# Queries and keys of one attention layer: normalised, scaled, turned and saved group by group in one pipeline

## What is computed

```python
x = x + _L0_attn_ref(_layernorm(x), ...)
x = x + _L0_ffn_ref(_layernorm(x), ...)
qkv = _layernorm(x) @ qkv_w + qkv_b                     # 128 -> 3 * 128
q, k, v = jnp.split(qkv, 3, axis=-1)                    # 16 heads of 8 channels
q = q / (jnp.linalg.norm(q, axis=-1, keepdims=True) + 1e-06) * qn_scale + qn_bias
k = k / (jnp.linalg.norm(k, axis=-1, keepdims=True) + 1e-06) * kn_scale + kn_bias
for _ in range(2):                                      # the training steps
    grads = jax.grad(loss)(theta)      # loss = mean((swish(k @ gate) * (k @ val) @ proj - v) ** 2)
    theta = muon(theta, grads)
x = x + (swish(q @ gate) * (q @ val)) @ proj @ proj_w + proj_b
x = x + _L1_ffn_ref(_layernorm(x), ...)                 # eight experts, two for each token
```

## Time and profile before

| | us |
|---|---|
| three runs | 1463.47 median, 1460.00 to 1467.11 |
| the profiled execution, its own time | 1465.41 |
| its span, first to last instruction | 1463.7 |
| PE busy in the span | 1172.7 (80%) |
| DVE busy | 939.5 (64%) |
| ACT busy | 446.6 (31%) |
| POOL busy | 507.3 (35%) |
| mean granted clock of PE | 0.905 of 2.4 GHz |
| the stage of the change, first transpose to the first training matmul | 504.97 to 597.73 |

### The profile page before, as it was taken

The page is one execution under the profiler, slowest core; times in us unless marked ns, Lnnn a source line. Parts: engine busy times, 40 slices in busy tenths (PEclk is TensorE's granted clock), DMA queues, the critical chain, the costliest instruction groups (busy, mean ns, idle before and its releaser), DMA issues.

```text
span 1463.7 us, 16561 instructions
## 1 busy us (share of the span) xinstructions
PE 1172.7 (80%) x4825; PEld 699.6 (48%) x4825; DVE 939.5 (64%) x2037; ACT 446.6 (31%) x844; POOL 507.3 (35%) x461
## 2 busy tenths in 40 slices
PE   3899999905656564699999889999988997399990
PEld 1444444403345432355555555555555665277770
DVE  5787888775577699467667556766754665323324
ACT  3545444235322231222122322212232322133340
POOL 4788888922244156400000000000000366245552
PEclk9999999957977785699999999999999998599995
DMA  4312222000000003100008200000000112434415
GB/s 134 107 56 63 76 63 77 1 0 1 1 0 0 1 0 137 65 22 22 14 21 355 74 0 22 22 14 21 8 15 7 44 50 68 125 87 112 121 46 183
DMA packets 60188, 81.82 MB, mean 56 GB/s; under 512 B 8620, under 2 KB 34622, under 8 KB 59617
## 3 DMA queue, kind: packets, MB, share of 16 engines
q1 hardware_dynamic: 55201, 72.54, 15.6%
q0 software_dynamic: 4672, 8.55, 1.8%
q10 hardware_dynamic: 256, 0.03, 0.0%
HBM read 33.77 MB, written 31.99 MB: 45 GB/s over the span
## 4 chain that ended last, share of the span: by engine, by line
PE 65%; DVE 16%; issue 8%; POOL 4%; ACT 4%; DMA 1%; SPq 1%; DVEq 0%; POOLq 0%; ACTq 0%
PE banks L1516 45%; PE banks L1405 7%; PE banks L1551 2%; PE banks L1337 2%; PE banks L1338 2%; PE banks L1493 1%; DVE arena L1990 1%; PE banks L1467 1%; DVE X L1878 1%; PE banks L1346 1%; POOL arena L936 1%; DVE arena L1798 1%; ACT XN L1158 1%; POOL arena L971 1%; DVE q_small L649 1%
## 5 line engine op out<-in xcount | busy, mean ns | idle before, releaser
L1516 PE MATMUL banks<-arena 128*128 128x128 f32 (+4 forms) x1516 | 391.5, 397 | 7.6 <-DVE arena L2084 4.5
L1516 PEld LDWEIGHTS banks<-arena 128*128 128x128 f32 (+1 forms) x1516 | 208.8, 191 | 89.2 <-issue 61.6
L1405 PE MATMUL banks<-arena,ident 128*128 128x512 f32 x368 | 175.3, 609 | 10.3 <-DVE arena L1829 9.0
L1022 POOL IOTA arena<- 128x32 f32 x1 | 0.2, 205 | 510.2 <-DVE ttt_val_w L2091 510.2
L2029 DVE TENSOR_TENSOR arena<-banks,arena 128x512 f32<-128x512 f32 x64 | 44.2, 691 | 134.4 <-ACT arena L1228 134.4
L936 POOL TENSOR_TENSOR arena<-arena 128x512 f32<-128x512 f32 x96 | 112.2, 1195 | 16.8 <-ACT arena L1095 16.8
L1054 POOL DMA_INDIRECT expert_out_scratch<-arena x80 | 80.6, 1007 | 97.1 <-DVE arena L2286 76.0
L1405 PEld LDWEIGHTS banks<-arena,ident 128*128 128x128 f32 x368 | 67.7, 194 | 88.2 <-issue 64.9
L1829 DVE TENSOR_TENSOR arena<-arena,banks 128x512 f32<-128x512 f32 x152 | 96.1, 675 | 0.5 <-PE banks L1405 0.5
L943 POOL TENSOR_TENSOR arena<-arena 128x512 f32<-128x512 f32 x64 | 81.3, 1270 | 5.0
L1231 ACT ACTIVATE arena<-banks 128x512 f32<-128x512 f32 x64 | 38.2, 597 | 146.5 <-PE banks L1551 146.5
(11 more groups left out here) (316 smaller groups left out, 2122.7 us busy)
## 6 DMA issues: line engine op xcount, KB each, us to landing
arena<-arena SPq DMA_DIRECT2D x64, 224.0 KB
arena<-expert_in_scratch SPq DMA_DIRECT2D x16, 580.5 KB
expert_in_scratch<-arena SPq DMA_DIRECT2D x4, 1225.5 KB
expert_in_scratch<-arena SPq DMA_DIRECT2D x5, 967.5 KB
arena<-kT_scratch SPq DMA_DIRECT2D x16, 256.0 KB, 2.6
arena<-k_scratch SPq DMA_DIRECT2D x16, 256.0 KB, 2.6
arena<-in_L_ffn_W_dram SPq DMA_DIRECT2D x16, 256.0 KB, 3.0
arena<-expert_out_scratch SPq DMA_DIRECT2D x8, 512.0 KB, 6.8
```

The source lines that it names most:

```text
L1405: m = nc.tensor.matmul(bank[ACC[b % 2]][:], ident[:], src, start=first, stop=last)
L1516: return nc.tensor.matmul(out_, lhsT, rhs, start=start, stop=stop)
```

## The change

The three parts become one pipeline over iterations 0 to 11, written out without loops. In iteration i: VectorE adds the bias of group i and normalises group i-2 (`unit`: the seven small steps, now on 128 columns, and the wide multiply). ScalarE normalises the tiles of group i+1 (`normalised5`), copies them when turned, takes the root of group i-1, squares group i, copies out the turned key and query of group i-3 and the key of group i-4. TensorE multiplies group i, turns the key and query of group i-3 straight from `QK`, and turns the key of group i-4 back.

Scale and bias move behind the turn. There a channel is a partition, so that ScalarE's copy takes them as its scale and bias operands, from the four columns of `affine`. They are made once: four copies on VectorE into `tiled4`, four transposes, one small copy. Since k is now finished only in turned form, TensorE turns it back (bank 1) and ScalarE copies it to `kBs`, from where it is saved.

SP waits, before the first load, for the last group's saves to be issued but only for group 0's to have landed. POOL loses the two steps on the queries; its additions of `b_proj` follow the last head sums directly. `kTs`, `qTs`, `kBs` and `nrm` have space of their own. `xT5` turns through one bank (0) instead of two.

```diff
-        kTs = xs5
-        qTs = xT5
+        kTs = view(o5, 2, L)
+        qTs = view(o5 + 2 * L, 2, L)
+        kBs = view(o5 + 4 * L, 2, L)
+        nrm = view(o5, 2, 6, TPB * NH2)
+        tiled4 = view(o5, 4, P)
+        affine = sb("affine", P, 4)
...
@@ sync @@
-            by_pairs(sp, NB, save_qk)
-            for s in range(2):
-                for x in (k_saved, kT_saved, qT_saved):
-                    sp.wait_ge(x[s].sem, x[s].at(NB // 2))
+            for g in range(NB + 1):
+                if g < NB:
+                    save(kT_dram, kTs, kT_ready, kT_saved, g)
+                    save(qT_dram, qTs, qT_ready, qT_saved, g)
+                if g:
+                    save(k_dram, kBs, kB_ready, k_saved, g - 1)
...
+                    for g in range(NB):
+                        sp.wait_ge(kT_saved[g % 2].sem, kT_saved[g % 2].at(g // 2 + 1))
+                        sp.wait_ge(k_saved[g % 2].sem, k_saved[g % 2].at(g // 2 + 1))
+                        load_k(g, g % 2)
...
@@ gpsimd @@
-            def q_affine(g, s):
-                pool.tensor_tensor(out=qv, in0=qv, in1=q_scale[:].unsqueeze(1).unsqueeze(1).to_broadcast(sh), op=ALU.mult).then_inc(q_scaled.sem, q_scaled.unit)
-                pool.tensor_tensor(out=qS[:, s, :].rearrange("p (c h d) -> p c h d", c=TPB, d=HD), in0=qv,
-                                              in1=q_bias[:].unsqueeze(1).unsqueeze(1).to_broadcast(sh), op=ALU.add).then_inc(q_ready.sem, q_ready.unit)
-            by_pairs(pool, NB, q_affine)
...
@@ scalar @@
+            def turned_kq(g):
+                act.wait_ge(kqT_mm.sem, kqT_mm.at(2 * g + 1))
+                nc.scalar.activation(kTs[:, g % 2, :], bank[6][:], ACT.Identity, bias=affine[:, 1:2], scale=affine[:, 0:1]).then_inc(kT_ready.sem, kT_ready.unit)
+                act.wait_ge(kqT_mm.sem, kqT_mm.at(2 * g + 2))
+                nc.scalar.activation(qTs[:, g % 2, :], bank[7][:], ACT.Identity, bias=affine[:, 3:4], scale=affine[:, 2:3]).then_inc(qT_ready.sem, qT_ready.unit)
+            for i in range(NB + 4):
+                if i + 1 < NB:
+                    normalised5(i + 1)
+                    xT5_copy(i + 1)
+                if 1 <= i <= NB:
+                    root(i - 1)
+                if i < NB:
+                    squares(i)
+                if 3 <= i < NB + 3:
+                    turned_kq(i - 3)
+                if 4 <= i:
+                    turned_back(i - 4)
...
@@ tensor @@
+            for i in range(NB + 4):
+                if i < NB:
+                    pe.wait_ge(xT5_ready.sem, xT5_ready.at(i + 1))
+                    for j in range(TPB):
+                        if j == TPB - 1 and i + 1 < NB:
+                            xT5_transposes(i + 1)
+                        if i:
+                            pe.wait_ge(v_biased.sem, v_biased.at((i - 1) * TPB + j + 1))
+                        nc.tensor.matmul(bank[2 + j][:, 0:3 * D], xT5[:, i % 2, j * P:(j + 1) * P], w_qkv[:], start=True, stop=True).then_inc(qkv_mm.sem, qkv_mm.unit)
+                if 3 <= i < NB + 3:
+                    turn_kq(i - 3)
+                if 4 <= i:
+                    turn_k_back(i - 4)
...
@@ vector @@
+            for i in range(NB + 2):
+                if i < NB:
+                    bias_qkv(i)
+                if i >= 2:
+                    unit(i - 2)
```

More of the change, by code:

```diff
@@ L1187, in _, with normalised5 @@
             layernorm_root(act, 4)
-            def xT5_copy(g, s):
+            def normalised5(g):
+                if g >= 2:
+                    act.wait_ge(xT5_mm.sem, xT5_mm.at(g - 1))
+                for j in range(TPB):
+                    n = g * TPB + j
+                    nc.scalar.activation(xs5[:, g % 2, j * P:(j + 1) * P], X[:, n, :], ACT.Identity,
+                                         bias=shift[:, n:n + 1], scale=rstd[:, n:n + 1]).then_inc(ln["out"].sem, ln["out"].unit)
@@ L1217, in _, with root @@
[L1217 to L1221 removed]
+                nc.scalar.activation(SQ[:, g * TPB:(g + 1) * TPB, :], QK[:, g * TPB:(g + 1) * TPB, :], ACT.Square).then_inc(qk_squared.sem, qk_squared.unit)
+            def root(g):
+                act.wait_ge(sum_sq_ready.sem, sum_sq_ready.at(g + 1))
+                if g >= 2:
+                    act.wait_ge(nrm_step.sem, nrm_step.at(7 * (g - 2) + 2))
+                nc.scalar.activation(nrm[:, g % 2, 0, :], sum_sq[:, g * TPB * NH2:(g + 1) * TPB * NH2], ACT.Sqrt).then_inc(root_ready.sem, root_ready.unit)
@@ L1475, in _ @@
             m.then_inc(wpT_mm.sem, wpT_mm.unit)
+            pe.wait_ge(wide_made.sem, wide_made.at(4))
+            for i in range(4):
+                m = nc.tensor.transpose(bank[4][:, i * P:(i + 1) * P], tiled4[:, i, :], ident[:])
+            m.then_inc(affine_mm.sem, affine_mm.unit)
             pe.wait_ge(x2_ready.sem, x2_ready.at(NB))
             pe.wait_ge(wpT_ready.sem, wpT_ready.at(1))
-            def xT5_transposes(g, s):
+            pe.wait_ge(affine_ready.sem, affine_ready.at(1))
@@ L1485, in xT5_transposes @@
                 m.then_inc(xT5_mm.sem, xT5_mm.unit)
-            def qkv(g, s, last=False):
-                pe.wait_ge(xT5_ready.sem, xT5_ready.at(g + 1))
-                for j in range(TPB):
-                    if j == TPB - 1 and not last:
-                        xT5_transposes(g + 1, 1 - s)
-                    pe.wait_ge(v_biased.sem, v_biased.at((g - 1) * TPB + j + 1))
-                    nc.tensor.matmul(bank[2 + j][:, 0:3 * D], xT5[:, s, j * P:(j + 1) * P], w_qkv[:], start=True, stop=True).then_inc(qkv_mm.sem, qkv_mm.unit)
@@ L1510, in _, with turn_kq @@
-            by_pairs(pe, NB, transposes)
-            pe.wait_ge(kT_ready.sem, kT_ready.at(NB))
+            def turn_kq(g):
+                pe.wait_ge(unit_ready.sem, unit_ready.at(g + 1))
+                for part, (at_, to, done) in enumerate(((D, 6, kT_ready), (0, 7, qT_ready))):
+                    if g:
+                        pe.wait_ge(done.sem, done.at(g))
+                    for j in range(TPB):
+                        m = nc.tensor.transpose(bank[to][:, j * P:(j + 1) * P], QK[:, g * TPB + j, at_:at_ + D], ident[:])
+                    m.then_inc(kqT_mm.sem, kqT_mm.unit)
@@ L1939, in _ @@
                 nc.vector.bn_stats(stats[:, n, :], X[:, n, :]).then_inc(ln["stats"].sem, ln["stats"].unit)
+            for i, v in enumerate((k_scale, k_bias, q_scale, q_bias)):
+                nc.vector.tensor_copy(tiled4[:, i, :].rearrange("p (h d) -> p h d", d=HD), v[:].unsqueeze(1).to_broadcast([P, H, HD])).then_inc(wide_made.sem, wide_made.unit)
             add_down(NB - 1)
@@ L2000, in _ @@
-            iteration = [None]
-            with dve.Fori(0, NB // 2) as i:
-                iteration[0] = i
-                for s in range(2):
-                    unit(2 * i + s, s)
+                dve.wait_ge(nrm_step.sem, nrm_step.at(7 * g + 6))
+                nc.vector.scalar_tensor_tensor(heads, m0, 1.0, r0, ALU.add, ALU.mult).then_inc(nrm_step.sem, nrm_step.unit)
+                dve.wait_ge(nrm_step.sem, nrm_step.at(7 * g + 7))
+                dve.wait_ge(qk_squared.sem, qk_squared.at(g + 1))
```

192 lines of the change are left out of this document (74 added, 118 removed).

## The result

| | us |
|---|---|
| changed kernel, five runs | 1454.33 median, 1451.32 to 1455.08 |
| kernel before, five runs beside it | 1464.32 median, 1460.00 to 1467.11 |
| ratio, 95% interval | 0.9929, 0.9911 to 0.9947 |
| profiled execution, its own time | 1452.28 (before 1465.41) |
| its span | 1450.2 (before 1463.7) |

The changed kernel is 0.71% faster; the forecast was 0.46%, 1456.8 us. By the medians the gain is 10.0 us, and the stage alone is 10.9 shorter. The profiled spans lie 13.5 apart: 10.9 from the stage, 0.7 from ahead of it and 1.9 from behind it, where nothing was changed. These last two are within the scatter of runs of one kernel (3.8 us for the changed one).

What follows compares the result with a forecast made beforehand. VectorE was taken to set the time from 536.6 to 588.2 us and SyncE's round trip through memory the rest. The first training matmul moves from 597.7 to 591.0, 6.7 us less, giving 1456.8 us, range 1446 to 1468.

Steps and rivals of the forecast that it cites:

- end of unit(7): VectorE's last normalisation, behind the last projection: forecast at 580.4 us, or 572.8 without POOL's additions beside it.
- last copy: ScalarE's copy of group 7's turned-back key, forecast 5.95 us after unit(7), at 586.4 us.
- The first groups: Start of the pipeline: group 0's last bias at 512.3 us, groups 1 and 2 at 4.7 us each, ending at 521.7.
- The period: Each later group on VectorE: 6.0 us of its own work plus 1.6 of blocking by POOL's head sums, 7.6 us.
- The end: Tail after group 7's bias: POOL's b_proj additions hold VectorE's unit(6) steps at 1.26 us each; ends 7.6 us apart.
- The choice between the page and the row: POOL beside VectorE: measured rows used; the skill's rule of mutual full blocking would end the sum 1.4 us later.
- Drain and load: After unit(7): 5.95 us to the last copy, then 4.6 through SyncE's save and loads to the training matmul at 591.0.
- Rival 1: VectorE and POOL's shared ports cost little: period 6.6 us, 5 + 7.6 us more gained, 1444 us; chance 0.22.
- Rival 2: TensorE stays at 1.2 GHz and bounds each group: period 10.2 us, 1472.8 us, 0.64% slower; chance 0.10.
- Rival 3: TensorE at a mixed clock of 0.77: period 8.5 us, 4.5 us later, 1461.3 us, no change; chance 0.12.
- forecast case: Whole kernel at 1456.8 us, 0.46% faster, with its own range 1452 to 1461 us; chance 0.56.
- the signs: Things to see in the changed profile: bias ends near 522 and 560 us, step times, TensorE's clock, first load at 587.

Runs made afterwards that it cites:

- e2: Changed kernel with the first two of POOL's three head sums taken for one head only; stage 75.58 us against 81.85.
- e6: Changed kernel with POOL's head sums moved beside VectorE's bias additions and ScalarE's root behind the squares; stage 76.14 us against 81.85.
- e1: Changed kernel with POOL's additions of b_proj waiting for the last unit; stage 74.75 us against 81.85.
- e8: Changed kernel with b_proj's additions last, head sums beside the biases and the turn back first; stage 68.01 us against 81.85, time 1504.89 us.
- e9: Changed kernel unaltered, run again beside the kernel before on another chip; stage 81.95 us, time 1513.76 us against 1525.14.
- e4: Changed kernel with all eight units behind the whole projection, lag 8 instead of 2; stage 83.33 us against 81.85.
- e3: Changed kernel with SyncE again waiting for all saves to land before the first load; stage 83.61 us against 81.85.

## Why the prediction was right, step by step

All positions here are from the first transpose (504.97 before, 504.27 after), so that the 0.7 us ahead of the stage does not count; the last column is each step's own part of the difference.

| step | forecast | measured | difference of the step |
|---|---|---|---|
| last bias of group 2 | 16.7 | 16.2 | -0.6 |
| last bias of group 7 | 54.7 | 52.6 | -1.6 |
| end of unit(7) | 75.4 | 72.35 | -0.9 |
| last copy | 81.4 | 77.7 | -0.6 |
| first training matmul | 86.0 | 81.85 | -0.5 |

**The first groups.** 4.45 us a group instead of 4.7: TensorE's and ScalarE's hand-overs were a little shorter.

**The period.** 7.28 instead of 7.6. VectorE's own work is 5.82 (6.0 in the sum) and the blocking 1.46 (1.6). The mechanism, the place (the first sum at the end of the reciprocal, the other two at dependent steps) and the size held; e2 and e6 show it by taking it away in two ways.

**The end.** The additions of b_proj hold unit(6) step by step, at 1.23 to 1.38 (1.26 forecast), and the forecast of L1006's length, 11.2, compares with 11.10. The block was 19.8 us instead of 20.7. e1 shows 7.1 us for it, the prediction had 7.6.

**The choice between the page and the row.** POOL lost 1.28 us beside VectorE (11.10 against 9.82 alone in e1). 1.0 of it is the multiply of group 5: the addition that it met took 2.25 instead of 1.28. The others took 1.28 to 1.32 and began 1.23 to 1.28 apart instead of 1.22, so that each of the six small steps that were held, which take 0.22 to 0.29 alone, cost POOL about 0.05. By the rule weighed in the prediction (the Trainium skill, SBUF — State Buffer, section SBUF: two separate sides: whoever starts first holds the ports and the other waits) they would have cost it their whole length, 1.7 together by their times alone (an estimate), instead of 0.3. The measured rows were the right guide: the rule fits what VectorE lost here, and for POOL it fits the wide multiply roughly and the small steps not.

**Drain and load.** 5.4 instead of 5.95 and 4.1 instead of 4.6. The turn of key and query together took 1.97 for eight transposes, where 2.2 was taken, and the save in front of the loads cost 0.2 of the 0.5 set for it: the matmul starts 3.2 after the second load is issued, 3.0 before.

**The rivals.** Rival 1 needed the sums beside nothing and the additions out of the way. Neither happened by itself, and with both made to happen (e8) the period was 6.45 against its 6.6. Rival 2 fell: from 521 to 541 us TensorE had 1.00, but for its end, where the clock fell. It fell in two stretches of 4 us; the two lines of the stretches have the columns of the earlier trace rows, the third is of the timeline:

```profile
541.00:545.00 4.00, 4.00 (x18) 3.47 (x17) 3.93 (x11) 2.70 (x4) 1.49 (x2) 0.66 0.03 11
553.00:557.00 4.00, 2.04 (x10) 2.04 (x11) 3.93 (x12) 0.45 (x2) 0.17 (x1) 0.62 0.32 119
...
539.49 0.66 PE L1510 MATMUL banks<-ident,arena 128*128 128x128 f32 x4 [2.90 <-ACT arena L1192]
```

In the first TensorE is busy all the time, and the period stays at 7.28, which VectorE sets: at the higher clock TensorE is busy for 4.3 us of a group (5.1 in the sum) and has 3 us to spare. Both falls came at the two longest waits of the pipeline, 2.90 us before 539.49 and 3.00 us before 554.96; the wait of 2.85 before 531.74 had none behind it. In e9, the same kernel, the clock fell in other groups, behind waits of 2.85 and 2.73, so the length of a wait alone does not tell. The Trainium skill (TensorE: Matmul & The Clock Gate, section HAM oscillation) has a kernel in which every burst behind a wait began at the lower clock; here some did, and most ran at 1.00, so the step from that page to rival 2 as the outcome does not hold. Rival 3 had the mixed clock (0.91 over the stretch) but not its effect.

**Where the sum was off.** All five steps were taken too long, by 0.5 to 1.6 us, and the errors have one sign: the gain of the stage was forecast at 6.7 and is 10.9. The largest is the period, 0.3 a group on five groups. Small hand-overs and bounds were each rounded up, and nothing was set against them. That made the difference between just inside and just outside of what can be told from no change. Errors of one sign did not cancel, so that the forecast case does not owe its place to luck; but the time came out closer (2.5 us) than the stage (4.2), because the medians of the two kernels lie 10.0 apart where the stage gives 10.9, and because the kernel before has 1464.3 beside the changed one where the forecast took 1463.5 for it. That part is scatter.

**What the signs said.** The bias of group 2 ended at 520.4 (near 522 forecast), that of group 7 at 556.8 (560), the first load of kT_scratch was issued at 582.5 (587). The wide multiply took 1.22 and once 2.17, the steps of unit(6) 1.23 to 1.38. Only the clock, forecast at 1.00 until 560, was wrong (it fell from 540 to 544 and again at 554), and it cost nothing in the period.

**What the prediction did not say.** It costed the parts forward and never asked which of them carries the gain. Undone one at a time they read: key's scale and bias on VectorE 11.1 us, the overlap 1.5 net (e4), SyncE's wait 1.8 (e3). Their sum, 14.4, is not the 10.9 of the whole: each was undone with the others in place, and the change also brings things that cost, the additions of b_proj 7.1 (e1) and the sums 5.7 (e6), so these numbers are no account that adds up. What the query's scale and bias on POOL would do in the pipeline was not tried, nor a clock held up through the tail.

## What to carry to other kernels

Where one engine bounds a stage in either order, a pipeline gives only the time in which that engine stood idle; first take operations off it, into scale and bias operands of a copy that is made anyway. When work of a second engine moves beside it, list each of that engine's steps, those queued behind as well, and give it a wait that puts it beside steps it doesn't hold: biases from PSUM, or the stage after.

## What was not expected of the hardware

- One-operand steps were held as well: L1999, a TensorScalar of 128 columns, took 1.29 us beside POOL's additions and 0.22 without them. The reciprocal took 0.95 beside both sums and additions, and biases from PSUM 0.42 and 0.28 beside the sums, as alone.
- The holding is one-sided for small steps: POOL's additions held six small steps of VectorE to their ends, and took 1.28 to 1.32 instead of 1.28; only the one that met the wide multiply took 2.25.
- ScalarE's copy from PSUM of 512 columns takes 0.77 with scale and bias from memory (L1216, L1219) and 0.60 without (L1224). The prediction had 0.6 for all three; the 0.33 a group lies on ScalarE's round, which did not bound.
- TensorE kept 2.4 GHz in e4 from 562 us on, through bursts of twelve transposes every 3.71 us with waits of 2.2 us between them. In e1 the same bursts at the same spacing, behind a wait of 5.75 us, ran at 1.2 GHz from 563.1 to the end of the drain (0.50 in every stretch), where they last longer and the waits between them are 0.9 us. So this pattern went on at whichever clock it had; what raised the clock in e4 at 561 was not examined.
